# Scaling by 1/deviation and gamma on GpSimd in the first stage of a four-layer graph network

## The reference

```python
x = x * node_weights[None, :, None] + node_bias[None, :, None] + x
h = jnp.einsum('bnf,fo->bno', x, W)
mu = jnp.mean(h, axis=-1, keepdims=True)
var = jnp.mean((h - mu) ** 2, axis=-1, keepdims=True)
h = (h - mu) * jax.lax.rsqrt(var + LN_EPS) * ln_gamma + ln_beta
residual = h
s1 = h @ a1
s2 = h @ a2
# then: leaky_relu of s1 + s2, masked softmax, product with h, + residual, elu
```

## Time and profile before

| | |
|---|---|
| median of 3 runs | 3748.92 us (3747.92 to 3750.82) |
| the profiled execution | 3749.33 us |
| its span, first to last instruction | 3747.2 us |
| mean granted TensorE clock over the span | 0.958 |
| busy over the span | PE 92%, DVE 83%, ACT 46%, POOL 47% |
| first stage | 0 to about 209 us of the span |

### The profile page before, as it was taken

The page is one execution under the profiler, slowest core; times in us unless marked ns, Lnnn a source line. Parts: engine busy times, 40 slices in busy tenths (PEclk is TensorE's granted clock), DMA queues, the critical chain, the costliest instruction groups (busy, mean ns, idle before and its releaser), DMA issues. The chain is left out here.

```text
span 3747.2 us, 60296 instructions
## 1 busy us (share of the span) xinstructions
PE 3452.9 (92%) x21147; PEld 1823.3 (49%) x21147; DVE 3114.5 (83%) x7053; ACT 1724.5 (46%) x3546; POOL 1771.8 (47%) x828
## 2 busy tenths in 40 slices
PE   5759999784999999999999999999996999699999
PEld 4659999651111111111111111111115999599999
DVE  6768888666999999999999999999965776477777
ACT  7811111371666666666666666666662444300100
POOL 2300000110888888888888888888891111000000
PEclk8779999895999999999999999999998999899999
DMA  6521221255011000111001110111003332211220
GB/s 233 187 103 59 84 85 52 92 230 195 5 28 28 28 19 16 28 28 28 10 23 29 28 28 5 28 28 29 5 5 103 114 113 80 112 48 52 91 79 30
DMA packets 59727, 240.72 MB, mean 64 GB/s; under 512 B 11696, under 2 KB 14128, under 8 KB 45232
## 3 DMA queue, kind: packets, MB, share of 16 engines
q1 hardware_dynamic: 59440, 236.91, 18.3%
HBM read 151.80 MB, written 85.07 MB: 63 GB/s over the span
## 5 line engine op out<-in xcount | busy, mean ns | idle before, releaser
L1337 POOL TENSOR_TENSOR a_w<-a_w,keep_mask_t 128x1024 f32<-128x1024 f32 x768 | 1632.4, 2151 | 353.6 <-ACT a_w L1322 353.6
L1322 ACT ACTIVATE a_w<-a_sc_ps 128x512 f32<-128x512 f32 x2048 | 1111.4, 595 | 780.8 <-PE a_sc_ps L1239 779.1
L1271 DVE CUSTOM_DVE_ANT_0 a_mx_ps<-a_mx_ps,a_mbias 128x512 f32<-128x512 f32 x2056 | 1352.5, 719 | 84.5 <-PE a_mx_ps L1196 71.6
L1212 PE MATMUL a_o_ps<-a_w,a_v 128*33 128x512 f32 x4096 | 1079.6, 605 | 7.2 <-POOL a_w L1337 7.0
L839 PE MATMUL g_acc<-g_hv,g_w 128*128 128x129 f32 x8192 | 923.6, 276 | 36.4 <-DVE g_w L776 24.0
L839 PEld LDWEIGHTS g_acc<-g_hv,g_w 128*128 128x128 f32 x8192 | 922.1, 193 | 38.1 <-DVE g_w L776 38.1
L776 DVE SCALAR_TENSOR_TENSOR g_w<-g_row,keep_s,keep_mask_t 128x1024 f32<-128x1024 f32 x512 | 647.2, 1282 | 202.6 <-PE g_acc L839 182.9
L1239 PE MATMUL a_sc_ps<-a_qs,a_ks 97*128 97x512 f16 x2048 | 622.1, 385 | 0.3
L1196 PEld LDWEIGHTS a_mx_ps<-a_ks,a_qs 32*128 32x128 f16 x2056 | 92.1, 91 | 850.1 <-DVE a_mx L1271 455.6
L1284 DVE TENSOR_TENSOR a_w<-a_w,keep_mask_t 128x1024 f32<-128x1024 f32 x256 | 460.7, 1800 | 28.4 <-ACT a_w L1322 28.4
L1196 PE MATMUL a_mx_ps<-a_ks,a_qs 32*128 32x512 f16 x2056 | 395.6, 392 | 52.8 <-DVE a_mx L1271 33.9
(11 more groups left out here) (198 smaller groups left out, 2163.3 us busy)
## 6 DMA issues: line engine op xcount, KB each, us to landing
h_nodes<-p_h SPq DMA_DIRECT2D x16, 1032.0 KB, 4.2
g_h<-h_nodes SPq DMA_DIRECT2D x16, 1032.0 KB, 6.2
p_adj_in<-in_adj SPq DMA_DIRECT2D x16, 1024.0 KB, 8.3
g_row<-u_rows SPq DMA_DIRECT2D x32, 512.0 KB, 7.4
p_x<-x SPq DMA_DIRECT2D x16, 1024.0 KB, 8.9
v<-p_v SPq DMA_DIRECT2D x8, 1056.0 KB, 6.9
a_v<-v SPq DMA_DIRECT2D x16, 528.0 KB, 3.6
p_x<-in_x SPq DMA_DIRECT2D x8, 1024.0 KB, 4.9
```

The costliest lines, as they stand in the source:

```text
L1212: mm = nc.tensor.matmul(o_ps[2 * HD * a:2 * HD * a + HD + 1, c % 2, :], v[u][:, jt, a, :], w[:, g % PB, a, :], start=(jt == 0), stop=(jt = ...
L1271: last = nc.vector.tensor_tensor_reduce(out=mx_ps[:, buf, a, :], in0=mx_ps[:, buf, a, :], in1=mbias[:, t, kc * BANK:(kc + 1) * BANK], scal ...
L1322: nc.scalar.activation(w[:, g % PB, a], sc_ps[:, n % SB], ACT.Exp, scale=SCALE).then_inc(exp_done, 1)
L1337: nc.gpsimd.tensor_tensor(w[:, g % PB], w[:, g % PB], keep["mask_t"][:, jt, c * BANK:(c + 1) * BANK].unsqueeze(1).to_broadcast([P, 2, BANK ...
```

## The change

GpSimd gets `scale_h`: two multiplies over the whole 128x2048, the first h0 times the inverse deviation (broadcast along the features), the second in place by gamma (broadcast along the tiles), with a wait for the first. It stands last in GpSimd's turn. ScalarE loses `norm_h`, VectorE the multiply by gamma; the addition of beta stays on VectorE and waits for GpSimd's second multiply (`h1_ready`). ScalarE waits for GpSimd's first (`gamma_done`) of an earlier batch before it overwrites `h0`. GpSimd waits once for the weights to be loaded.

```diff
+            def scale_h(b, k):
+
+                pool.wait_ge(rooted_h, b + 1)
+                pool.wait_ge(h_ready, b)
+                nc.gpsimd.tensor_tensor(h1[:], h0[k][:, :, 0:F], rstd_h[:].unsqueeze(2).to_broadcast([P, T, F]), ALU.mult).then_inc(gamma_done, 1)
+                pool.wait_ge(gamma_done, b + 1)
+                nc.gpsimd.tensor_tensor(h1[:], h1[:], gamma[:].unsqueeze(1).to_broadcast([P, T, F]), ALU.mult).then_inc(h1_ready, 1)
+
             def turn(b, k, half):
                 if not first(b):
                     root_h(b - 1)
                 if not late(b):
                     root_x(b + 2)
+                if not first(b):
+                    scale_h(b - 1, 1 - k)
...
+            pool.wait_ge(weights_in, 16 * 7)
             batches(pool, turn)
             root_h(B - 1)
+            scale_h(B - 1, 1)
...
             def affine(b):
                 dve.wait_ge(h1_ready, b + 1)
-                nc.vector.tensor_tensor(h1[:], h1[:], gamma[:].unsqueeze(1).to_broadcast([P, T, F]), ALU.mult).then_inc(gamma_done, 1)
-                dve.wait_ge(gamma_done, b + 1)
                 dve.wait_ge(h_stored, 16 * b)
...
-            def norm_h(b, k):
-                act.wait_ge(rooted_h, b + 1)
-                act.wait_ge(h_ready, b)
-                for t in range(T):
-                    ins = nc.scalar.activation(h1[:, t, :], h0[k][:, t, 0:F], ACT.Copy, scale=rstd_h[:, t:t + 1])
-                ins.then_inc(h1_ready, 1)
-
...
                 if not first(b):
                     act.wait_ge(scores_kept, 2 * (b - 1))
+                    act.wait_ge(gamma_done, b - 1)
...
-                if not first(b):
-                    norm_h(b - 1, 1 - k)
...
             batches(act, turn)
-            norm_h(B - 1, 1)
```

## The result

The changed kernel takes 3771.73 us in the median of six runs (3768.07 to 3774.80) against 3749.62 for the kernel before (3747.40 to 3753.51): a ratio of 1.0059, with a 95% interval of 1.0046 to 1.0071. It is 22.1 us slower; 29.0 were forecast.

The account below looks back on a forecast made before the run. The first stage was taken as bound by two nearly equal rings, ScalarE with TensorE and VectorE with GpSimd; the change lengthens the second. Turns 1 to 7 and the tail add 29.04 us to 3749.33, giving 3778.4, range 3769 to 3795.

Parts of the forecast that it names:

- The ring: First stage: VectorE and GpSimd wait for each other in turn with nothing overlapping; full turn 26.20 us against 20.4.
- the price: Time of one wide multiply on GpSimd, taken as 4.26 us, twice the attention masking's median of 2.128.
- the path through the multiplies: From `root_x`'s end to the beta addition: two multiplies of 4.26 us plus gaps of 0.1, 0.24 and 0.05, together 8.91.
- The covers: First stage: ScalarE's later start, loads, stores and small VectorE operations beside the multiplies cost nothing, at most 1.8 us.
- the 4.8 of cover: Batch b+1 is normalised about 16.9 us after `root_x` ends; the next `root_x` needs it 21.7 after: 4.8 us spare.
- the 1.8 allowed for them: `scores`, 0.6 us in turns 6, 7 and the tail, could end up behind the second multiply: at most 1.8 us.
- the first three: Rivals pricing each wide GpSimd multiply at 2.29 us (3746.8, chance 0.04), 1.80 (3739.0, 0.03), or up to 6.22 (above 5.3: 0.07).
- the fourth: Rival: TensorE's clock falls to 0.5 and ScalarE with TensorE sets the turn; up to 10.4 us, 3788.8; chance 0.08.

Follow-up runs that it names:

- e3: Changed kernel, but ScalarE waits for the first multiply only ahead of `keep_h0`, and GpSimd starts that multiply only after `shift_of_x`: 3774.22 us, 1.0067 to before.
- e5: Changed kernel with the gamma multiply put back on VectorE, ahead of the beta addition; GpSimd keeps the inverse-deviation multiply: 3756.03 us, 1.0017 to before.
- e1: Changed kernel with `scale_h` ahead of `root_x` in GpSimd's turn: 3758.97 us, 1.0029 to before.
- e2: Changed kernel with `scale_h` ahead of `root_x` on GpSimd and also `affine` ahead of `shift_of_x` on VectorE: 3751.67 us, 1.0008 to before.
- e7: Changed kernel with e3's edits, `affine` and the store of h one turn later, and VectorE's and SyncE's loops written out: 3742.57 us, 0.9984 to before.
- e4: Changed kernel with the multiplies' operands exchanged, gamma first (h0 into h1), then the inverse deviation in place: 3771.45 us, run once.

## Why the prediction was right

**The ring.** The step that decided was that `scale_h` stands behind `root_x` and `affine` behind both. In the changed kernel's full turns the waits of VectorE and GpSimd are the ones that were worked out, in that order: of the 8.8 us forecast for VectorE's wait behind `root_x`, 4.6 stand in the record as idle time and 3.6 as a held `shift_of_x`. e3 excludes ScalarE as the holder, e5 shows that the price counts one for one, and e1 and e2 show that the place is the cause. Forecast and measured, from `stats_h` to `stats_h` (us):

| | forecast | measured |
|---|---|---|
| start of turn 2 | 76.79 | 76.25 |
| turns 2 to 5 | 104.80 | 101.88 |
| turn 6 | 20.15 | 19.56 |
| turn 7 | 18.08 | 17.47 |
| tail | 18.08 | 17.46 |
| stage longer by | 29.04 | 23.77 |

**The size.** The whole difference is one term, the path through the multiplies: 8.91 us forecast, 8.21 measured (from the end of `root_x` at 65.83 to the start of the beta addition at 74.04), in each of eight batches, 5.6 us in all, for a difference of 5.3. Of the 0.70, 0.39 is the price: 3.60 and 4.53, together 8.13, for twice 4.26. The nearest row, twice the attention's masking, lay between the two: 0.66 too dear for one and 0.27 too cheap for the other. That the two errors partly cancel is luck; nothing in the forecast told the two multiplies apart. The other 0.31 are gaps put too high: GpSimd starts the second multiply 0.08 us after the first has ended and not 0.24, and the first one without the 0.1 allowed. The rows of the first batch, GpSimd's and then VectorE's:

```profile
62.93 2.90 POOL L101 TENSOR_TENSOR p_rstd_x<-p_tmp_x,p_minus_half 128x16 f32<-128x16 f32 x1 [8.89 <-ACT p_hn L442]
65.80 3.61 POOL L269 TENSOR_TENSOR p_h<-p_h,p_rstd_h 128x2048 f32<-128x2048 f32 x1
69.48 4.53 POOL L271 TENSOR_TENSOR p_h<-p_h,p_gamma 128x2048 f32<-128x2048 f32 x1
```

```profile
74.04 2.29 DVE L351 TENSOR_TENSOR p_h<-p_h,p_beta 128x2048 f32<-128x2048 f32 x1 [4.61 <-POOL p_h L271]
```

By the Trainium skill's 4497 ns for an f32 `tensor_tensor` of 2048 elements (GPSIMD Engine Reference, section "3.1 Elementwise — side-by-side cycle accounting") the gamma multiply is hit (4.53) and the other missed by 0.9; the sum would have been further off than by the trace's row.

**The covers** (what the forecast put at nothing because other work hides it). ScalarE was forecast to start 4.5 us after `root_x`, it starts 3.7 after it (120.65 against 116.91) and normalises until 133.10, where the next `root_x` starts at 137.88: the 4.8 of cover are there. `shift_of_x` is held by the first multiply and, as allowed for, costs nothing. Of `scores` in turn 6, L341 runs for 0.18 and L342 is held for 3.59 by the first multiply; VectorE still waits 4.46 for the second one afterwards, so the 1.8 allowed for them were not spent.

**The rivals.** None of the first three's prices came: the two multiplies take 4.07 on average, far from 2.45, the point where the sign turns, and from 5.3. TensorE's clock, in the fourth, stood at 0.73 to 0.80 in the full turns, where it was 0.74 and 0.75, and in those turns no wait of VectorE or GpSimd ends with TensorE or ScalarE.

What the prediction didn't see is that the hold-ups it priced at nothing are harmless only here, since VectorE has nothing else to do beside the multiplies. In e1 and e2 the chain stands 6.6 us in a turn, and the turn is 1.9 and 2.4 us longer than worked out without.

## What to carry over

An idle share is no room: before giving an engine work, look which instruction on it comes just before and which on the other engines waits just behind, in program order. Here 8.2 us of work on an engine idle for 11 cost 5 a turn at the end of the ring, 2 with a better place, and nothing once its consumer stood a turn later. When operations move to GpSimd, look at every small VectorE operation beside them: each one with two SBUF inputs, and in e7 also some with one, can last until the GpSimd one ends.

## What the hardware showed unexpectedly

- A multiply of 128x2048 f32 on GpSimd takes 3.61 us if one operand repeats along the innermost axis, 4.53 in place and 4.16 from another buffer (e4, eight multiplies of one execution) if it repeats along the outer one. The starts of what follows agree with these durations: 3.68 from one multiply to the next (65.80 to 69.48), 4.56 to the beta addition (74.04).
- VectorE's operations of 128x16 with two SBUF inputs, 0.17 us alone, lasted up to 4.5 us, to within 0.1 us of the end of GpSimd's multiply. So did one with a single tensor input and constants (a `TENSOR_SCALAR` of 128x16 f32 in e7, 89.59 to 94.05, beside a multiply that ended at 94.03). So did the biases of turn 6 (`TENSOR_SCALAR` in bf16, 3.99 us for 0.69). `BATCH_NORM_STATS2` was not held: sixteen took 3.18 us in e7 (from 105.87) beside a first multiply (106.03 to 109.64).
- It works in the other direction too: `root_x` and `root_h` took 4.4 to 5.0 us where `m01` or the beta addition had started just ahead of them and 2.90 without. Where `root_x` started first (e7, 102.48, `m01` at 102.89), it took 3.25 and `m01` its usual 1.90. In e7 a multiply of 3.61 took 5.14 where an `m01` had started ahead of it.

VectorE's timeline in e7, the held operation and that `m01`:

```profile
89.59 4.46 DVE L333 TENSOR_SCALAR p_tmp_h<-p_tmp_h 128x16 f32<-128x16 f32 x1
...
159.71 1.90 DVE L303 TENSOR_SCALAR p_m<-p_adj_in 128x2048 bf16<-128x2048 int32 x1
```

GpSimd's timeline in e7 beside them:

```profile
89.50 4.53 POOL L270 TENSOR_TENSOR p_h<-p_h,p_gamma 128x2048 f32<-128x2048 f32 x1
...
159.93 5.14 POOL L268 TENSOR_TENSOR p_h<-p_h,p_rstd_h 128x2048 f32<-128x2048 f32 x1 [0.31 <-DVE p_h L350]
```
